# A two-layer gated attention kernel: plain scores in banks of their own from the fourth sequence on, first maxima kept in PSUM, layer 1's products and the feed-forward input reordered

## What is computed

```python
x = x + tanh(g_xattn[0]) * L0_attention(layernorm(x), ctx)      # 16 heads of 8, causal mask
x = x + tanh(g_ffn[0])   * L0_ffn(layernorm(x))                 # quantized input and weights, 512 wide
x = x + tanh(g_xattn[1]) * L1_attention(layernorm(x), ctx)      # each head sees every 16th token
x = x + tanh(g_ffn[1])   * L1_moe(layernorm(x))                 # 16 experts, top 2, and a shared one

# layer 0's attention, per sequence and head
scores = where(mask, q @ k.T / sqrt(8), -inf)
out = softmax(scores) @ v
# layer 0's quantized input
scale = 127 / max(|x|, per token);  xq = round(x * scale) / scale
```

## Time and profile before

| | |
|---|---|
| median of 3 runs | 175.5 us (174.81 to 176.05) |
| profiled execution, device time | 175.18 us |
| its span, first to last instruction | 173.1 us |
| PE busy | 157.0 us (91%) |
| DVE busy | 122.9 us (71%) |
| ACT busy | 79.8 us (46%) |
| POOL busy | 42.1 us (24%) |
| granted TensorE clock | 1.000 in the mean over the span |
| chain that ended last | PE 65%, DVE 14%, ACT 11%, issue 5% |

### The profile page before, as it was taken

The page is one execution under the profiler, slowest core; times in us unless marked ns, Lnnn a source line. Parts: engine busy times, 40 slices in busy tenths (PEclk is TensorE's granted clock), DMA queues, the critical chain, the costliest instruction groups (busy, mean ns, idle before and its releaser), DMA issues.

```text
span 173.1 us, 5045 instructions
## 1 busy us (share of the span) xinstructions
PE 157.0 (91%) x2106; PEld 109.4 (63%) x2114; DVE 122.9 (71%) x354; ACT 79.8 (46%) x138; POOL 42.1 (24%) x62
## 2 busy tenths in 40 slices
PE   7878999999999889885787899999999989999993
PEld 5545768766667566574555668475776755757572
DVE  6589376856887978789796896759576686644453
ACT  1356685644655446873849641556122312221210
POOL 7834609975050000190050016000020000000000
PEclk9999999999999999999999999999999999999999
DMA  4997000000000000000000000000000000100001
GB/s 127 410 312 325 4 4 6 4 6 6 4 4 4 4 0 4 0 2 4 0 0 0 4 0 0 0 2 4 0 0 0 0 4 2 61 0 0 0 0 61
DMA packets 1895, 5.90 MB, mean 34 GB/s; under 512 B 209, under 2 KB 593, under 8 KB 1745
## 3 DMA queue, kind: packets, MB, share of 16 engines
q1 hardware_dynamic: 1152, 4.01, 6.3%
q10 hardware_dynamic: 720, 1.57, 2.5%
HBM read 5.06 MB, written 0.52 MB: 32 GB/s over the span
## 4 chain that ended last, share of the span: by engine, by line
PE 65%; DVE 14%; ACT 11%; issue 5%; DMA 2%; POOL 1%; DVEq 0%; ACTq 0%
PE banks L1411 10%; PE banks L1436 10%; PE banks L1414 10%; PE banks L1163 4%; PE banks L1140 3%; ACT pT L478 3%; PE banks L1238 2%; DMA x_all<-in_x 2%; PE banks L1202 2%; DVE banks L770 2%; PE banks L1424 2%; ACT ffn_work L554 2%; ACT f_hqT L560 2%; PE banks L1051 2%; PE banks L1134 2%
## 5 line engine op out<-in xcount | busy, mean ns | idle before, releaser
L1436 PEld LDWEIGHTS banks<-ews,rest 128*128 128x128 f32 x160 | 20.6, 191 | 7.8 <-issue 7.7
L770 DVE TENSOR_REDUCE banks<-banks 128x4 f32<-128x512 f32 (+1 forms) x32 | 16.5, 561 | 11.2 <-PE banks L1170 11.1
L1051 PE MATMUL banks<-idle 128*128 128x256 bf16 x158 | 22.2, 286 | 1.2 <-DVE idle L677 1.2
L654 ACT ACTIVATE full<-banks 128x512 f32<-128x512 f32 x20 | 11.9, 593 | 21.9 <-PE banks L1411 21.9
L1436 PE MATMUL banks<-ews,rest 128*128 128x128 f32 x160 | 21.0, 275 | 0.0
L1411 PE MATMUL banks<-nT,ews 128*128 128x512 f32 x40 | 20.6, 597 | 0.2
L1009 DVE TENSOR_TENSOR xnT<-full,banks 128x512 f32<-128x512 f32 x20 | 13.7, 683 | 9.6 <-PE banks L1414 7.3
L1414 PE MATMUL banks<-nT,ews 128*128 128x512 f32 x40 | 20.4, 592 | 0.0
L280 POOL TENSOR_SCALAR ve<-mv 128x4 f32<-128x4 f32 x8 | 2.0, 256 | 73.3 <-DVE mv L684 73.3
L1051 PEld LDWEIGHTS banks<-idle 128*128 128x128 bf16 x158 | 16.0, 103 | 4.8 <-DVE idle L677 1.2
L1021 DVE TENSOR_TENSOR rest<-xnT,banks 128x512 f32<-128x512 f32 x20 | 13.7, 687 | 5.2 <-remote 2.6
(11 more groups left out here) (182 smaller groups left out, 314.3 us busy)
## 6 DMA issues: line engine op xcount, KB each, us to landing
ews<-in_ew SPq DMA_DIRECT2D x1, 1928.5 KB, 8.3
fws<-in_fw SPq DMA_DIRECT2D x1, 768.0 KB, 7.9
cT<-in_ctxT ACTq DMA_DIRECT2D x2, 256.0 KB, 5.5
x_all<-in_x SPq DMA_DIRECT2D x2, 256.0 KB, 4.7
lws<-in_lw ACTq DMA_DIRECT2D x1, 449.0 KB, 8.4
sels<-in_sel ACTq DMA_DIRECT2D x1, 320.0 KB, 8.7
a<-in_aw ACTq DMA_DIRECT2D x1, 256.0 KB, 5.0
out_x<-x_all SPq DMA_DIRECT2D x1, 256.0 KB, 2.0
```

The lines of the kernel that those rows point to most:

```text
L654: nc.scalar.activation(e_sil[:, k % 2, :], bank[k % 2][:, :], ACT.Silu).then_inc(sm["e_silr"], 1)
L770: V.tensor_reduce(group_max(p)[:, u, :, :], scored[:, :, :, keys], AX.X, ALU.max).then_inc(sm["a_mx"], 1)
L1051: mm(bank[t][:, 0:2 * S], idle[:, 0:128], idle[:, :], start=True, stop=True)
L1436: last = mm(bank[t][:, b * D:(b + 1) * D], e_h[:, u, b * S:(b + 1) * S], expert(c)[2], start=(c == 0 and (b == 0 or s == 1 and b == 2)), s ...
```

## The change

From step n = 3 (`SPLIT`) on, the plain scores of either half go to banks 4 and 5, and only the transposed ones stay in banks 0 to 3. DVE's maxima then go to a tile of SBUF (`gmax`). `score_masks(n, p)` now waits for the reductions of the half before (a_mx), and `transposed_masks(n, p)` for `exp(n-1, p)`. From (2, 1) on the rows of maxima lie in a free part of the first bank of the half's own pair. In all steps `mT` holds 128 columns where it held 192 (the late queries stood there twice), so `max_rows` makes four matmuls of 64 columns, and `subtract_max` sixteen, of 128 and 64 columns.

`layer1_proj(0)` and `(1)` leave the loop and stand at the start of the feed-forward, with their copies and `own_tokens` behind; `keys_times_queries` and `values_times_outputs` follow later, those for s = 1 in the place of two `keep_busy`, and another `keep_busy` (8 matmuls) goes. `x_quantize(0)` moves on DVE ahead of `heads_out(6)`, and `xqT_copy(0)` on ACT ahead of the table load for Silu.

```diff
+        gmax = sb("gmax", [128, 2, 2 * HG])
-        mT = sb("mT", [128, PW], BF16)
+        mT = sb("mT", [128, S], BF16)
-        J_RAW, J_KQ, J_VO = 8, 10, 12
+        J_RAW, J_KQ, J_VO = 8, (10, 12), (11, 13)
+        def score_pair(n, p):
+            return 2 if n >= SPLIT else p
...
-            for s in range(2):
-                own_tokens(0, s)
-                own_tokens(1, s)
+            nc.gpsimd.memset(wT[:, :], 0.0).then_inc(sm["wT_zero"], 1)
             rstd_of(1, 0)
+            own_tokens(0, 0)
+            own_tokens(1, 0)
             rstd_of(1, 1)
...
             last.then_inc(sm["f_xn1"], 1)
+            own_tokens(0, 1)
+            own_tokens(1, 1)
...
+                if n == SPLIT and p == 0:
+                    pe.wait_ge(sm["proj_out"], J_V[1] + 1)
+                    pe.wait_ge(sm["w_mean"], 1)
+                elif n >= SPLIT:
+                    pe.wait_ge(sm["a_mx"], 4 * n + 2 * p)
+                elif n:
                     pe.wait_ge(sm["a_exp"], 2 * (n - 1) + p + 1)
...
                 for w in range(2):
-                    for j in (2 * p, 2 * p + 1):
-                        for t in range(2):
-                            last = mm(bank[j][side(t), w * PW:(w + 1) * PW], minus[strip(j), 2 * w + t, :],
-                                      mT[strip(j), :], start=False, stop=True, skip_group_check=True)
-                        if w == 1:
-                            last.then_inc(sm["a_T"], 1)
+                    for first, queries in ((0, slice(0, S)), (S, slice(HB, S))):
+                        for j in (2 * p, 2 * p + 1):
+                            for t in range(2):
+                                at = w * PW + first
+                                last = mm(bank[j][side(t), at:at + queries.stop - queries.start],
+                                          minus[strip(j), 2 * w + t, :], mT[strip(j), queries],
+                                          start=False, stop=True, skip_group_check=True)
+                            if w == 1 and first:
+                                last.then_inc(sm["a_T"], 1)
...
             gate_up(0)
+            gate_up(1)
+            layer1_proj(1)
             y_proj(B - 1)
-            gate_up(1)
-            keys_times_queries(1)
             gate_up(2)
+            keys_times_queries(0)
+            gate_up(3)
             values_times_outputs(0)
-            pe.wait_ge(sm["proj_out"], J_KQ + 2)
-            keep_busy(0, 8)
-            gate_up(3)
-            values_times_outputs(1)
-            pe.wait_ge(sm["proj_out"], J_VO + 1)
+            pe.wait_ge(sm["proj_out"], J_RAW + 1)
             h_transposes(0)
...
             gate_up(4)
             h_transposes(2)
-            keep_busy(0, 3)
+            keys_times_queries(1)
             gate_up(5)
             h_transposes(3)
-            keep_busy(0, 4)
+            values_times_outputs(1)
             down(2)
             down(3)
+            pe.wait_ge(sm["proj_out"], J_VO[1] + 1)
             keep_busy(0, 6)
```

More of the change, by code:

```diff
@@ L470, in max_copy @@
                 rows = slice(64 * p, 64 * p + 64)
-                nc.scalar.activation(mT[rows, :], maxima_bank(n)[rows, 2 * S:2 * S + PW], ACT.Copy)\
+                nc.scalar.activation(mT[rows, :], maxima(n, p), ACT.Copy)\
                     .then_inc(sm["a_mTs"], 1)
@@ L541, in xqT_copy @@
                                      ACT.Copy).then_inc(sm["f_xqTs"], 1)
+            xqT_copy(0)
+            nc.scalar.activation(table[:, 0:1], tg[:, 0:1], ACT.Silu)
             def silu(n):
@@ L1192, in max_rows @@
                 pe.wait_ge(sm["a_mid"], 2 * n + p + 1)
[L1193 to L1195 removed]
+                apart = maxima_apart(n, p)
+                if n >= 2 and p == 0 and apart:
                     pe.wait_ge(sm["a_res"], n - 1)
[L1197 to L1207 removed]
+                rows = maxima(n, p)
+                for u, out in ((0, rows[:, HB:S]), (1, rows[:, 0:HB])):
+                    for t in range(2):
+                        last = mm(out, mxs[:, p, u, 4 - 4 * t:68 - 4 * t], identb[:, side(t)],
+                                  start=(apart and u == 0 and t == 0), stop=True, skip_group_check=True)
                 last.then_inc(sm["a_mT"], 1)
@@ L1262, in _ @@
             k_proj(1)
-            for n in range(1, B):
+            for n in range(1, SPLIT):
                 score_masks(n, 0)
@@ L1294, in _ @@
                     q_proj(1)
-                elif n == 2:
-                    layer1_proj(0)
+            for n in range(SPLIT, B):
+                score_masks(n, 0)
+                transposed_masks(n - 1, 1)
+                late_scores(n, 0)
+                early_keys(n - 1, 1)
+                early_scores(n, 0)
+                late_keys(n - 1, 1)
+                max_rows(n - 1, 1)
+                heads(n - 1, 0)
+                y_proj(n - 2)
+                subtract_max(n - 1, 1)
+                score_masks(n, 1)
+                transposed_masks(n, 0)
+                late_scores(n, 1)
+                early_keys(n, 0)
+                early_scores(n, 1)
+                late_keys(n, 0)
+                max_rows(n, 0)
+                heads(n - 1, 1)
+                subtract_max(n, 0)
             transposed_masks(B - 1, 1)
-            max_rows(B - 1, 1)
             early_keys(B - 1, 1)
             late_keys(B - 1, 1)
-            y_proj(B - 2)
+            max_rows(B - 1, 1)
+            heads(B - 1, 0)
             subtract_max(B - 1, 1)
-            heads(B - 1, 0)
-            heads(B - 1, 1)
             def xq_transposes(s):
@@ L1314, in xq_transposes @@
                 last.then_inc(sm["f_xqTp"], 1)
-            pe.wait_ge(sm["proj_out"], J_KQ)
             xq_transposes(0)
-            keys_times_queries(0)
+            layer1_proj(0)
+            y_proj(B - 2)
+            heads(B - 1, 1)
             def gate_up(n):
```

102 lines of the change are left out of this document (48 added, 54 removed).

## The result

The changed kernel takes 174.43 us (median of 15 runs, 173.36 to 175.28), the one before 175.92 in as many runs beside it (174.81 to 177.27). The ratio is 0.990, with an interval of 0.988 to 0.992. So 1.5 us are gained where 4.4 were forecast, and the time lies outside the range.

The account below looks back on a forecast made before the run. It took a loop of waits between PE, DVE and ACT to bound the attention's step at 6.15 us. 175.18 - 5.0 (attention, tail) + 0.6 (feed-forward) = 170.8, and 0.3 for the median: 171.1 us, range 169.9 to 173.9.

Parts of the forecast that it names:

- PE's step: Attention: with the loop of waits cut, a step is PE's load alone, some 5.4 us in place of 6.15.
- The subtraction: Attention on PE: 16 matmuls in place of 8 stream the same columns, +0.03 us each time, bounds 0 and +0.27.
- Steps 3 and 4: Attention: bound by PE, from 30.4 to 41.8 us, 6.0 and 5.4 us long, 0.6 lost in step 3.
- DVE as the bound behind step 4: Attention: DVE fuller than PE, 5.7 + 6.0 + 5.7 plus 0.5 of waits, first quantization ending at 61.1 us.
- the tail: End of the attention: first feed-forward product on DVE at 64.95 in place of 69.96, 5.0 us won up to there.
- the giveback: Feed-forward: 0.1 us lost at POOL's normalization and 0.5 behind the values for s = 1, 0.6 given back.
- the sum of 170.8: Whole kernel: profiled execution of 175.18, less 5.0 won, plus 0.6 given back, 170.8 us.
- the sentence on POOL: Feed-forward: POOL's roots for sequences 4 to 7 begin 0.4 late, normalization ends as DVE asks, 0.1 us lost.
- the clock rival: PE's gaps in the feed-forward lower its clock to 1.2 GHz, low into the experts; 7 us give 178; chance 0.05.
- The dearer subtraction: Rival, attention on PE: 34 ns per matmul, +0.27 us per subtraction, +2.9 in all, 173.9 us; chance 0.13.
- The single bank pair as a new loop: Rival, attention: 4.9 us a step, the old period if handoffs add 1.2, then 174.9 us; chance 0.07.
- More given back by POOL's late picks: Rival, feed-forward: picks, roots and normalization 1.8 us late, delaying DVE's second quantization as much, 172.9 us; chance 0.13.

Follow-up runs that it names:

- e1: Changed kernel with 28 fillers in place of 9 on PE ahead of the transposes of the second quantized input; 172.48 us, ratio 0.981.
- e2: Changed kernel with POOL's last two picks of tokens waiting for the end of DVE's second quantization, no filler added; 170.78 us, ratio 0.972.
- e8: e2 with the values for s = 1 and `gate_up(6)` back behind `down(3)`, six fillers there left out; 170.68 us, ratio 0.970.
- e5: Kernel before the change with two more picks of tokens on POOL, result unused, beside DVE's second quantization; 178.25 us, ratio 1.013.
- e6: e2 with the first quantization set back behind `heads_out(6)` on DVE, as in the kernel before; 173.07 us, ratio 0.982.
- e4: Changed kernel with SPLIT = 8, so plain and transposed scores share banks in all steps, the rest kept; 177.23 us, ratio 1.008.
- e7: Changed kernel, picks left in place, with the quantization's three 128x4 tensor_scalars each done as four 128x1 columns; 174.34 us, ratio 0.992.

## Why the prediction was wrong

**Right: the attention.** *PE's step*, forecast some 5.4 us, is 5.44. *The subtraction* +0.03: +0.02. *Steps 3 and 4*, 11.4 us, took 42.34 - 30.90 = 11.44, and from the first reduction of step 5 to the end of the quantization 17.9 were planned and 61.63 - 43.68 = 17.95 measured. All of it lies 0.5 us later than planned. Most of that is an accident of this one execution: the masks at 20.35 are level with the kernel before (20.33), those at 24.18 are 0.34 behind (23.84), and between them the heads' matmuls at 22.30 take 0.90 us where e1, the same program up to there, has 0.51. Step 3 begins at 30.90 in it, and at 30.41 in e1 and 30.60 in e2, for 30.4 planned. DVE as the bound behind step 4 came as forecast: 5.77 us for step 5, 6.14 for step 6 and 6.04 from 55.59 to the end of the quantization, for 5.7, 6.0 and 5.7 with 0.5 of waits; its waits were 0.23 and 0.37. What I had wrong is that PE's steps would show it. Steps 5 and 6 stayed at 5.44 on PE, which was ahead, and the plain masks wait for DVE in step 7 alone (0.44), where I had put it.

**Right: the tail**, minus those 0.5: first product on DVE at 65.65 for 64.95, 4.3 us won for 5.0. Its last 0.2 is output projection 6: `heads_out(6)` was done at 62.91, but the product of layer 1, which I had lying in that wait, ran on PE until 63.10.

**Right, as far as e2 shows it: the giveback.** I said 0.1 and 0.5 for the feed-forward. From the first product to the second quantization 69.96 to 77.87 became 65.35 to 73.30 in e2, under 0.1 more. Behind it, where nothing else disturbs, DVE waits 1.23 us for `down(2)` where it waited 0.68: the 0.5. The 4.6 us won at the first product (69.96 to 65.35) are 4.0 at residual 2 (85.33 to 81.33): 0.6 as forecast. e8 didn't get the 0.5 back, for with its order the copy behind the values ends last.

That e2's profiled execution, 170.88 us, meets the sum of 170.8 is in part luck. Its span is 169.1 us where the kernel before had 173.1: 4.0 us won, for 4.4 forecast. The other 0.3 lies outside the span, 1.8 us of device time in e2 and 2.1 before, and I had forecast nothing there.

**Wrong: what stands beside the second quantization.** The step that failed is the sentence on POOL, "the 3.13 us of normalization behind them end just when DVE asks: 0.1 lost". I followed POOL's work as far as DVE waits for it and stopped. The next two instructions on POOL, the picks for s = 1, are awaited by nobody for long, so I costed them at nothing ("All behind stays shifted"); but they run beside DVE's quantization, and an instruction can be slowed by one it doesn't wait for. Today's quantization takes 2.31 us with POOL at rest, and I carried that row to a place with another neighbour. It became 4.02: +1.7 us, gone in e2 and made anew in e5.

The Trainium skill ("SBUF — State Buffer", Who interferes with whom) has the rule: DVE and GpSimd share one pair of SBUF ports, as an exclusive lock, so that an instruction of DVE that wants the pair waits until GpSimd's instruction is over. Every tensor_scalar held here ended 0.01 to 0.03 us behind the end of a pick, and agrees; that the columns weren't held is not in the rule as I read it. The rule should have been a rival of its own.

**Wrong: the clock rival had the right mechanism, and the wrong reason against it.** I gave it 0.05 because "the gaps left are no longer than today's". That followed from the quantization at 2.31 us. At 4.02 the gap is 2.24 us, the clock falls for 6.8 us, and 2.0 us (medians) go with it (e1). The two errors are one: a stretch of 1.7 us on DVE cost 3.7 at the end. What the clock takes differs between executions of one kernel. In those of the kernel after the mean clock is 0.98 or 0.99, and the two groups lie 1.2 us apart; in e6 four executions with 0.99 took 173.05 to 173.52 us, and two with 1.00 171.83 and 171.99. So the same program can have a low stretch that is longer, shorter or absent, and a forecast of such a kernel has that as a spread of its own. How long the gap was in the executions without a trace isn't known. In the prediction's own sum for this rival, the gain over the median of 175.5 is gone from 4.4 us of it on; the 4.1 is measured from the profiled execution.

**The other rivals.** The dearer subtraction: 0.02 for 0.27. The single bank pair as a new loop: no, a step is 5.44. More given back by POOL's late picks: its roots started at 68.99 for the 68.3 planned, 0.7 late where all else was 0.5 to 0.7 late. The normalization ended at 73.61 and the quantization started at 73.64, 0.20 us after the start of DVE's instruction ahead of it where that was 0.11 before: the 0.1 of the forecast. This rival asked who waits for POOL, and not who works beside it.

## What to carry to other kernels

When work of POOL moves, lay it against what DVE does in that time, and not only against who waits for it: two 1.5 us instructions, which nobody needed soon, took 1.7 us from a chain, and one wait on POOL gave it back. Where a chain feeds PE, price a delay twice, once as itself and once as the gap that it leaves on PE: here 1.7 us of delay brought another 2.0 us of loss by the half clock. And if an edit's gain is seen up to some point of the trace and not behind it, compare the start and the end of each piece of the chain from there, since the piece that grew is then plain to see.

## What the hardware showed

- *Which instructions of DVE are held by a tensor_tensor of POOL.* Held until it ended: tensor_scalar on 128x4 float32, as small as it is (0.17 us to 0.74 and 2.00; 0.20 to 1.33; after, e1, e4, e5). Held up as well: a tensor_tensor on 128x512 with two inputs in SBUF (0.69 to 1.31 in e7, ending 0.55 behind the pick). Not held: tensor_scalar on 128x1 (eight in 1.03 us, with or without picks), reciprocal on 128x4 (0.18), tensor_reduce on 128x512 (0.69).
- *A held instruction doesn't get in between two picks as a matter of course.* In the kernel after L818 ended at 75.10, with the first pick (75.07) and not the second (76.53); in e5 the same one was held over both, 2.00 us. What decides it, no run shows.
- *The clock.* With PE idle for 0.51 and 0.69 us (e2), for 0.45 and 0.92 (before), or for 1.03 (e7, at 62.14), it stayed at 2.4 GHz. Behind idle times of 2.24, 2.28, 2.21, 2.01 and 1.35 us (after, e5, e4, e7, e6) it fell to 1.2 GHz in the profiled execution of each; of the other executions, two of e6 and one of e7 have a mean clock of 1.00. It fell when PE was working again, 0.3 us after it had resumed at 77.80 in the kernel after (low from 78.1 on), and 2.2 us after it had resumed at 80.40 in e4 (low from 82.6 on). It stayed low for 6.8 us in the kernel after and for some 3.4 in the others. 28 filler matmuls of 3.2 us in all, 19 more than the kernel has, kept it up and were worth 2.0 us.
- *Short matmuls on packed tiles.* Sixteen of 128 and 64 columns went at 18 ns each, eight of 192 at 34. Both stream 1536 columns, in 0.29 and 0.27 us: for this pair the time went with the columns, not with the number.
